# A transformer block on one core: the next stage's first rows and weights made in the stage before, and feed-forward's outputs summed in place in a ring of four

## What is computed

```python
def _layernorm(x, axis=-1, eps=1e-05):
    m = jnp.mean(x, axis=axis, keepdims=True)
    v = jnp.var(x, axis=axis, keepdims=True)
    return (x - m) / jnp.sqrt(v + eps)
...
    x = x + _L0_xattn_ref(_layernorm(x, axis=-1), ctx_768, L0_xattn_w_q, L0_xattn_w_k, L0_xattn_w_v, L0_xattn_w_o, L0_xattn_b_o)
    x = x + _L0_attn_ref(_layernorm(x, axis=-1), L0_attn_w_attn, L0_attn_w_proj, L0_attn_decay_raw)
    x = x + _L0_ffn_ref(_layernorm(x, axis=-1), L0_ffn_w1, L0_ffn_b1, L0_ffn_w2, L0_ffn_b2)
```

## Time and profile before

| | us |
|---|---|
| median of 3 runs | 1787.55 |
| lowest, highest | 1786.06, 1789.83 |
| profiled execution, device time | 1789.76 |
| its span on the core | 1788.0 |
| TensorE busy | 1660.3 (93%) |
| VectorE busy | 1165.1 (65%) |
| ScalarE busy | 1007.2 (56%) |
| GpSimd busy | 796.1 (45%) |

### The profile page before, as it was taken

One profiled execution on the slowest core, in us unless ns is written; L12 is line 12 of the kernel. 1 busy time (PEld: TensorE's weight loads), 2 busy tenths in 40 slices (PEclk: granted clock), 3 DMA queues, 4 the chain that ended last, 5 costly groups with the idle time before them and its releaser, 6 DMA issues. The chain is left out here.

```text
span 1788.0 us, 30494 instructions
## 1 busy us (share of the span) xinstructions
PE 1660.3 (93%) x11523; PEld 1442.9 (81%) x11523; DVE 1165.1 (65%) x2117; ACT 1007.2 (56%) x1966; POOL 796.1 (45%) x745
## 2 busy tenths in 40 slices
PE   6999999999999999999999988999975888989897
PEld 5888889898888998889888777988863676868685
DVE  5546676666666676676665854666645996868676
ACT  3346676666666666676665413444434665646554
POOL 3216455354554535455352321333333765554544
PEclk9999999999999999999999998999986999989999
DMA  7852222213222222322322841111113211010001
GB/s 251 243 171 65 78 76 66 87 56 97 66 75 77 70 82 67 93 61 78 98 78 88 290 141 54 37 54 54 43 39 110 94 54 59 13 59 6 30 18 36
DMA packets 103189, 148.11 MB, mean 83 GB/s; under 512 B 10434, under 2 KB 67842, under 8 KB 103044
## 3 DMA queue, kind: packets, MB, share of 16 engines
q1 hardware_dynamic: 103044, 146.17, 25.8%
HBM read 108.38 MB, written 37.75 MB: 82 GB/s over the span
## 5 line engine op out<-in xcount | busy, mean ns | idle before, releaser
L75 PE MATMUL p_bank_score<-p_ctxt,p_qo 128*128 128x256 f32 x2304 | 305.8, 287 | 6.9 <-DVE p_ctxt L1029 6.9
L75 PEld LDWEIGHTS p_bank_score<-p_ctxt,p_qo 128*128 128x128 f32 x2304 | 289.3, 192 | 12.7 <-DVE p_ctxt L1029 8.8
L75 PE MATMUL p_bank_mix<-p_probt,p_ctx 128*128 128x512 f32 x1152 | 296.0, 401 | 0.6
L75 PEld LDWEIGHTS p_bank_mix<-p_probt,p_ctx 128*128 128x128 f32 x1152 | 206.9, 189 | 41.6 <-issue 3.8
L1053 DVE SCALAR_TENSOR_TENSOR p_qo<-p_bank_mix,p_odd,p_qo 128x512 fp32r<-128x512 f32 x192 | 144.2, 751 | 104.4 <-ACT p_qo L904 104.4
L1741 PE MATMUL p_bank_down<-p_w,p_ht 128*128 128x512 f32 x768 | 194.3, 404 | 8.7 <-DVE p_ht L1841 8.7
L75 PE MATMUL p_bank_up<-p_zt,p_w 128*128 128x512 f32 x768 | 193.4, 402 | 1.4 <-DVE p_zt L158 1.4
L904 ACT ACTIVATE p_qo<-p_bank_mix,p_odd 128x512 fp32r<-128x512 f32 x192 | 132.2, 689 | 103.5 <-PE p_bank_mix L75 103.5
L890 ACT ACTIVATE p_probs<-p_bank_score,p_small 128x257 f32<-128x257 f32 x256 | 121.8, 476 | 118.6 <-DVE p_small L1036 117.2
L1700 POOL TENSOR_TENSOR p_a<-p_a,p_g 128x512 f32<-128x512 f32 x64 | 112.1, 1751 | 160.5 <-ACT p_a L1785 160.5
L1741 PEld LDWEIGHTS p_bank_down<-p_w,p_ht 128*128 128x128 f32 x768 | 146.5, 193 | 45.2 <-issue 10.1
(11 more groups left out here) (238 smaller groups left out, 3538.0 us busy)
## 6 DMA issues: line engine op xcount, KB each, us to landing
p_ctx_in<-in_ctx_dram SPq DMA_DIRECT2D x64, 384.0 KB, 3.2
q<-p_ctx SPq DMA_DIRECT2D x64, 256.0 KB, 3.0
p_odd_in<-in_ctx_dram SPq DMA_DIRECT2D x64, 192.0 KB, 3.5
p_x<-x SPq DMA_DIRECT2D x48, 256.0 KB, 3.1
p_x<-in_x_dram SPq DMA_DIRECT2D x32, 256.0 KB, 4.2
p_quad<-q SPq DMA_DIRECT2D x32, 256.0 KB, 3.8
p_probt<-q SPq DMA_DIRECT2D x32, 256.0 KB, 3.7
p_o_in<-o SPq DMA_DIRECT2D x8, 1024.0 KB, 6.5
```

Source lines behind the costliest of these rows:

```text
L75: made = e.matmul(out, lhsT, rhs, start=n == 0, stop=n == last)
```

## The change

`FirstRows` (p4a) lives over cross-attention's end and self-attention's start. Its loads of x1 stand at n = 2, 4, 6, 8 on SP, `scale` on GpSimd at n = 5, 7, 9, 11, `turn` on TensorE at n = 6, 8, 10, 12, `high` on ScalarE and `low` one tile later on VectorE; `guard` and `finish` cover the first four tiles only (parts of a table of 16), `root` stands at g = 2. The identity is made once. `FirstProducts` (p5a) lives over self-attention and feed-forward: tiles 16 to 19 of the same row pipeline are the first four of feed-forward, from x2, and turn at t = 12 to 15; the first 512 columns of w1 are loaded and split at t = 7 to 10 by ScalarE and GpSimd. Feed-forward has 28 blocks left: two ahead of the steps and two a step from step 0. Tiles for the next group stand at f = 3, 4, 5 (load, scale, turn) and every third step after. At a group's end x comes into a ring of four, GpSimd writes the sum into x's tile, the store reads that, and `raw[i % 2]` is free when GpSimd has added (`y_done`), not when the store has landed (`y_gone`). Outputs 0 and 1 are copied at the end of a step on VectorE, 2 and 3 after the next m. The bias matmul of each bank stands ahead of that bank's products.

```diff
+class FirstRows:
...
+        self.zts = room.ring("zt", 2, [P, 2, C // P, self.group], F32R)
...
+    def place(self, i):
+        tiles = self.group // P
+        return self.zts[i // tiles % 2], i % tiles * P
...
+class FirstProducts:
...
+        self.early = 4
+        self.w1 = room.sb("w1", [P, 2, C // P, C], F32R, side="right")
+        self.zt = room.sb("zt", [P, 2, C // P, self.early * P], F32R, side="right")
...
+        AHEAD = range(ahead.early)
+        loaded_at, scaled_at_tile, turned_at_tile = ({k + d * i: i for i in AHEAD} for k, d in ((2, 2), (5, 2), (6, 2)))
...
+                    if n in loaded_at:
+                        i = loaded_at[n]
+                        e.wait_ge(x1_gone[i % 3], DMA * (i // 3 + 1))
+                        if i >= 3:
+                            e.wait_ge(ahead.norm.chain, i - 2)
+                        e.dma_start(ahead.xs[i % 3][:], x1_dram[i * P:(i + 1) * P, :]).then_inc(ahead.x_in[i % 3], DMA)
...
+                if n in scaled_at_tile:
+                    i = scaled_at_tile[n]
+                    e.wait_ge(ahead.x_in[i % 3], DMA * (i // 3 + 1))
+                    ahead.norm.scale(e, i, ahead.xs[i % 3][:])
...
+                    if n in turned_at_tile:
...
+                        ahead.norm.turn(e, turned_at_tile[n])
...
+                if g == 2:
+                    ahead.norm.root(e, 0)
+                for n in range(g * NX, (g + 1) * NX):
+                    if n in turned_at_tile:
+                        ahead.norm.high(e, turned_at_tile[n], *ahead.place(turned_at_tile[n]))
...
+                    if n == ahead.early - 1:
+                        e.wait_ge(x1_seen, 2 * (n + 1))
+                        ahead.norm.guard(e, 0)
+                    if n == ahead.early:
+                        ahead.norm.finish(e, 0)
+                    if n - 1 in turned_at_tile:
+                        ahead.norm.low(e, turned_at_tile[n - 1], *ahead.place(turned_at_tile[n - 1]))
...
+        SEEN, WEIGHTS = 6, range(7, 7 + KT)
...
         def sync(e):
             def load_x(i):
-                if i >= 3:
...
             def load_y(i):
                 if i >= 3:
...
+            for i in range(ahead.early, ahead.early + 3):
...
             for t in range(NT):
...
+                if t + 7 < NT + after.early:
+                    load_x(t + 7)
+                if t + 2 in WEIGHTS:
+                    k = t + 2 - WEIGHTS[0]
+                    if k == 0:
+                        e.wait_ge(made, 7)
+                    else:
+                        e.wait_ge(after.w_lo, k)
+                    e.dma_start(w_raw[:], w_1[k * P:(k + 1) * P, 0:C]).then_inc(after.w_in, DMA)
                 e.wait_ge(added, t + 1)
                 e.dma_start(x2_dram[t * P:(t + 1) * P, :], ys[t % 3][:]).then_inc(y_out[t % 3], DMA)
...
+                if t in WEIGHTS:
+                    k = t - WEIGHTS[0]
+                    e.wait_ge(after.w_hi, k + 1)
+                    e.tensor_tensor(after.w1[:, LO, k, :], w_raw[:], f32(after.w1[:, HI, k, :]),
+                                    ALU.subtract).then_inc(after.w_lo, 1)
...
+            def turn_rows(i):
...
+                    norm.turn(e, i)
+                    return
+                if i == NT:
+                    e.wait_ge(norm.lo, NT)
...
+                if t == SEEN:
+                    after.norm.root(e, 0)
...
+                if t in WEIGHTS:
+                    k = t - WEIGHTS[0]
+                    e.wait_ge(after.w_in, DMA * (k + 1))
+                    e.activation(after.w1[:, HI, k, :], w_raw[:], ACT.Copy).then_inc(after.w_hi, 1)
...
+                if t == SEEN:
...
+                    after.norm.guard(e, 0)
+                if t == SEEN + 1:
+                    after.norm.finish(e, 0)
...
-        zts = room.ring("zt", 2, [P, 2, KT, G], F32R)
+        xs = room.ring("x", 4, [P, C])
+        zts = [ahead.zt, room.sb("zt", [P, 2, KT, G], F32R)]
...
+        def first_weights(s, k, f):
+            return ahead.w1[:, s, k, f * P:(f + 1) * P] if f < KT else w1[:, s, k, (f - KT) * P:(f - KT + 1) * P]
...
+        EARLY = 2
...
+            if c > 0:
+                blocks += [(w_1[k * P:(k + 1) * P, c * C:(c + 1) * C], w1[:, :, k, (c - 1) * C:c * C])
+                           for k in range(KT)]
...
+        def blocks_at(n, lane):
+            return [k for k in range(EARLY + 2 * n, min(EARLY + 2 * n + 2, len(blocks))) if lane in (None, k % 2)]
...
+        def tile_at(n, first):
+            g, f = divmod(n, KF)
+            return [(g + 1) * NR + (f - first) // 3] if n < NT and g + 1 < NG and f >= first and (
+                f - first) % 3 == 0 and (f - first) // 3 < NR else []
...
+        LOADED, SCALED, TURNED = 3, 4, 5
+        def done_at(n):
+            return [(n - LAG) // KF] if n >= LAG and (n - LAG) % KF == KF - 1 else []
...
             def load_x(n):
                 kind, i = x_uses[n]
...
                     if was == "z":
...
                     else:
-                        e.wait_ge(y_done, j + 1)
...
+                        e.wait_ge(y_gone[j % NR], DMA * (j // NR + 1))
...
             def store(i):
                 e.wait_ge(y_done, i + 1)
-                e.dma_start(out_rows[i * P:(i + 1) * P, :], raw[i % 2][:]).then_inc(y_gone[i % 2], DMA)
...
+                e.dma_start(out_rows[i * P:(i + 1) * P, :], x_of("y", i)).then_inc(y_gone[i % NR], DMA)
             load_block(0)
             load_block(1)
...
             for part in (0, QUAD):
                 e.dma_start(b2[part:part + 1, :], b_2[None, :]).then_inc(b2_in, DMA)
-            load_block(2)
...
+                for done in done_at(n):
+                    for i in range(NR):
                         load_x(at)
                         at += 1
...
+                    for i in range(NR if n == NT + LAG - 1 else 2):
+                        store(done * NR + i)
+                for i in tile_at(n, LOADED):
                     load_x(at)
                     at += 1
...
+                for done in done_at(n - 1):
+                    for i in range(2, NR):
+                        store(done * NR + i)
+                for k in blocks_at(n, None):
                     load_block(k)
...
             def output(i):
...
                 e.wait_ge(y_round, i + 1)
...
-                e.tensor_tensor(raw[i % 2][:], raw[i % 2][:], xs[at % 3][:], ALU.add).then_inc(y_done, 1)
...
+                x_is_in(e, "y", i)
+                e.tensor_tensor(x_of("y", i), raw[i % 2][:], x_of("y", i), ALU.add).then_inc(y_done, 1)
...
+            low_block(1)
             for n in range(NT + LAG):
...
+                for done in done_at(n):
+                    for i in range(NR if n == NT + LAG - 1 else 2):
+                        output(done * NR + i)
+                for done in done_at(n - 1):
+                    for i in range(2, NR):
+                        output(done * NR + i)
...
                     e.wait_ge(norm.lo, NR * (g + 1))
-                if g == 0 and f % 4 == 0:
-                    blocks_are_split(e, 8 * (f // 4) + KT)
+                if g == 0 and f % KT == 0 and f > 0:
+                    blocks_are_split(e, 2 * f)
...
             def down(n):
                 g, f = divmod(n, KF)
                 if g == 0:
-                    blocks_are_split(e, 8 * (f // 4) + KT + f % 4 + 1)
+                    blocks_are_split(e, 2 * (f - f % KT) + f % KT + 1)
                 if n == 0:
                     e.wait_ge(b2_ready, 1)
                     e.wait_ge(consts, 6)
-                if f == 0:
...
+                e.wait_ge(h_lo, n + 1)
+                for i in range(NR):
+                    if f == 0:
                         if g > 0:
                             e.wait_ge(y_round, (g - 1) * NR + i + 1)
                         e.matmul(b_down[i], ones[:], b2_pair[:], start=True, stop=False)
-                e.wait_ge(h_lo, n + 1)
-                for i in range(NR):
                     for j, (lhsT, rhs) in enumerate(three(
                             lambda s: ht[n % 2][:, s, i * P:(i + 1) * P], lambda s: w2[:, s, f, :])):
                         made = e.matmul(b_down[i], lhsT, rhs, start=False, stop=f == KF - 1 and j == 2)
...
+            norm.root(e, 1)
+            e.wait_ge(consts, 6)
+            e.activation(scratch[:], quarter[:], ACT.Gelu).then_inc(ready, 1)
+            for k in range(EARLY):
                 high_block(k)
-            e.wait_ge(consts, 6)
             e.wait_ge(b2_in, 2 * DMA)
             e.activation(b2_pair[0:1, :], b2[0:1, :], ACT.Copy).then_inc(b2_hi, 1)
             e.activation(b2_pair[QUAD:PAIR, :], b2[QUAD:PAIR, :], ACT.Copy).then_inc(b2_hi, 1)
...
             def output(i):
                 e.wait_ge(downed, NR * KF * (i // NR) + NR * (KF - 1) + i % NR + 1)
                 if i >= 2:
-                    e.wait_ge(y_gone[i % 2], DMA * (i // 2))
+                    e.wait_ge(y_done, i - 1)
                 else:
...
+            norm.prepare(e, 1)
```

(11 more changed lines are left out.)

298 lines of the change are left out of this document (132 added, 166 removed).

## The result

The changed kernel takes 1744.49 us in the median (1743.03 to 1747.36) against 1787.2 for the kernel before on the same chip: 0.9761 of it, with a 95% interval from 0.9743 to 0.9779. The profiled execution has a span of 1741.2 us, 46.8 under the span of before. The forecast was 1738.8 in a range from 1731 to 1752; by the spans of the two profiled executions, which the sum was made against, -48.8 was forecast and -46.8 came. That pair flatters the forecast: it sets one of the slower executions of before (1789.76, where they lie from 1786.06 to 1789.83) against the fastest of the changed kernel (1743.03). By the medians of before and after the gain is 42.7 us. So the total was nearly right, but its terms were not.

A forecast was written before the change was run, and what follows sets the result against it. TensorE, busy for 93% of the span, was taken as the bound, with gains only in its gaps. -10.8 + 1.4 + 0.3 + 2.6 - 18.5 - 21 - 2.8 = -48.8 gave span 1739.2, median 1738.8 us, range 1731 to 1752.

The forecast's parts named there:

- Part 1, the start: Self-attention's start: first rows made in cross-attention remove turns and waits, with 3.4 us added for low clock; -10.8 us.
- Part 1, the price in cross-attention: Cross-attention's last 16 tiles: four added turns cost +1.4 us, VectorE's added splits and normalization chain +0.3.
- Part 2: Self-attention's tiles 12 to 15: four added turns for feed-forward's first rows cost +2.6 us, between 1.4 and 4.
- Part 3, first m: Feed-forward's start: m(0) 8.5 us after the engines leave the boundary (T0), behind b2's split; -17.95 us.
- Part 3, the pace behind it: Feed-forward's first group: VectorE is full, steps stay between 5.6 and 6.7 us; a gain of 0.6 us in all.
- Part 4, ends of groups: Three feed-forward group ends: output 2's copy waits for GpSimd's add, 8.5 us an end instead of 15.1; -21 us.
- a wait of 1.67 leaves the clock full: Feed-forward's group ends: after so short a TensorE wait, the 12 matmuls behind it take 3.00 us.
- Part 5, tail: Kernel's end: with x already loaded, the last four adds of 1.26 us follow one another; -2.8 us.
- B: Group ends keep their gap because GpSimd's adds come late and the clock falls; 21 becomes 10, 1750 us, 15%.
- C: Feed-forward's start: biases late by +3.3 to +5 us, m(0) at T0 + 12 or 13; 1743 us, 10%.
- E: Feed-forward's first group: TensorE stays at half clock throughout, +61 us; 1799.5 us, slower than before, 2%.
- D: Tiles that take the moved work stall, by VectorE beside GpSimd's splits or the attention output's split; +4 to 5, 1743 us, 6%.

The follow-up runs named there:

- hold_start: The changed kernel with TensorE held at self-attention's start until the mask's logarithms are there, about 7.7 us later; 1752.88 us, ratio 0.9791.
- bias_first: The changed kernel with b1 loaded in self-attention's stage, and splits of b2 and the first two weight blocks moved behind the first m; 1746.41 us.
- by_need: The changed kernel with feed-forward's weight blocks reordered: groups of four w1 blocks one or two steps earlier, w2 blocks later; 1743.14 us, ratio 0.9734.
- pool_lane: by_need with three of four weight blocks split by GpSimd instead of two; 1755.31 us, ratio 0.9812.
- warm: The changed kernel with 40 matmuls whose result nobody reads in TensorE's gap ahead of the first down-product; 1746.76 us, ratio 0.9771.
- store_wait: The changed kernel with VectorE's copy of outputs 2 and 3 waiting again for the store of outputs 0 and 1; 1760.29 us, ratio 0.9832.

## Why the prediction was right, and which steps of it failed

The mechanisms were right in the main, but that the total came so near is in part luck, since the misses cancel. In the rows of the table cross-attention came 2.3 us better than forecast (-0.6 for +1.7), self-attention's start 3.1 and its middle 1.9; feed-forward's start with its first group came 2.8 worse (-15.7 for -18.5), and the ends with the tail 6.4 worse (-17.4 for -23.8).

- **Part 1, the start: mis-sized, 3.1 us too small.** -10.8 was forecast and -13.9 came. The step that failed is the 3.4 us added for half clock; the clock stayed full behind a gap of 3.2 us. In executions where it fell it cost 1.8. hold_start shows that an 11 us gap costs no more (1.3). The bound of -11.5 was too tight.
- **Part 1, the price in cross-attention: mis-sized.** Forecast 1.4 + 0.3; 2.5 over the eight tiles. There was the turn's 0.36 each, a short wait (0.22 for the split at 1021.71) and a slower tile behind each turn (4.37 for 18 matmuls instead of 4.24). The rest of the first row of the table, some 3 us the other way, lies in a thousand microseconds of unchanged work: with the same code the boundary came at places up to 3.8 us apart in twelve profiled executions (1064.60 to 1068.44).
- **Part 2: about right; the +0.7 has luck in it.** +2.6 forecast (1.4 to 4), +0.7 measured. The last projection ran at half clock before (4.57 us) and at full clock in this execution (3.04); by that alone feed-forward starts 1.5 us earlier. In bias_first, by_need, pool_lane and warm the projection takes 4.4 to 4.6 us again, and scores to boundary 242.4 us, 2.7 over before. Without this the stage costs 2.3 here. The two turns in full tiles cost 0.5 each (15.06 us a tile instead of 14.58), and the last two turns 0.6 together and not 1.8, since TensorE waits there. Each of nine middle tiles takes 15.06 instead of 14.98 us, and no run here says why. ScalarE's extra table loads and GpSimd's splits stay hidden, as forecast.
- **Part 3, first m: right, but one wait was missing.** T0 + 8.1 against 8.5, behind b2's split as forecast. The sum put the landing of b2 at T0 + 6.5 as what ScalarE waits for. It waited for the second weight block instead, up to 1333.96, and began b2 at T0 + 6.0 without a wait; so the two nearly alike times are chance. On ScalarE the two loads stand at 1328.47 and 1329.99 and the next operation follows 1.30 us after the start of the second. The Trainium skill, ScalarE: Activation LUTs, section "What ACT_TABLE_LOAD costs", gives 2.66 us with the drain; no drain shows in these rows, and the measurement decides.
- **Part 3, the pace behind it: the wrong sign.** Forecast -0.6, measured +2.7. The step that failed took VectorE's pace as the only limit. The later stream of blocks made TensorE wait before steps 8 and 12 (by_need gives back 1.7), and the gap of 9.3 us, where before only one up-product ran at half clock (5.23), put the first down with its biases and most of an up-product there (warm gives back 1.0 at most).
- **Part 4, ends of groups: mechanism right, size 5 us too good.** -21 forecast; -17.8 measured from up-product to up-product, -16.0 with the up-product behind each end. Step: 8.5 us an end, against 9.15. The wait was 1.0 and not 1.7, but the biases cost 0.43 each, 1.7 and not 1.2, and some 0.8 more lies where they alternate with the products (three matmuls and then a bias: 0.89 us, where a quarter of 2.80 is 0.70). And the third end lost 1.25 us to the clock, and 1.8 in the up-product behind it, which the step "a wait of 1.67 leaves the clock full" had excluded. Each of the twelve profiled executions with this ending has one or two such ends, 16 of 36; nine have one of 10.2 to 10.8 us. The working gave all of the gain to the release; by store_wait that is 12.2 of 16.0 us. The last row of the table is still 1.6 us short: the steps between the ends are a little longer, in the last group 5.60 instead of 5.56 us, and no run says why.
- **Part 5, tail: right.** From the last down-product's start to the end 12.2 us before, 9.2 after: -3.0 against -2.8.
- **The rivals.** B (GpSimd's adds late) didn't come: the adds start right behind GpSimd's last step of the Gelu (1459.62). C is excluded by m(0), E by the clock of 0.98 in the second stretch. D came in its smallest form.

## What to carry to other kernels

Work moved ahead of a boundary is worth the whole chain that stood behind it, and here it cost a sixth of that, because the stage ahead had idle engines beside a full TensorE. Cost each moved stream by when its last block is needed and not by its amount: the loads that went from before the first step into the steps came late twice. Where a buffer's release waits for a store, write the sum into the tile that is stored, and put work on other buffers ahead of the instruction that waits.

## What the runs showed that I had not expected

- Behind a gap of 3.2 us the granted clock is a matter of the execution: 120 matmuls in 17.85 to 18.1 us or in 19.65 to 19.76, with the same instructions. A gap of 1.01 us at a group's end left it full twice and lowered it once in the same execution. Where the low clock falls on the last projection of a stage, nothing hides it: 1.5 us.
- Idle matmuls keep the clock (first down in 5.4 us and not 9.0), and gain only where TensorE is the limit: at most 1.0 us at one place and none that these runs resolve at the other.
- One more block of four for GpSimd cost 7.7 us in the first group, though in the changed kernel GpSimd was busy for only 55.4 us of 84 there: a step is a chain over three engines, and a share of busy time doesn't show its length.
